# Two standalone norm stages dissolved: statistics in the routing and attention stages, the norm itself inside the zone stages

## The reference, cut to what matters

```python
def _layernorm(x):                       # over the 128 features, no gain, no bias
    return (x - mean(x)) / sqrt(var(x) + 1e-5)

def _L0_ffn_ref(x, W1, b1, W2, b2, Wa, Wb):
    pooled = x.mean(axis=1)              # over the 256 tokens of a sample
    h = tanh(pooled @ W1 + b1)
    probs = softmax(h @ W2 + b2)
    top_p, top_i = top_k(probs, 3)       # 3 of 8 zones for each sample, weights w
    for e in range(8):
        zone_outputs += (gelu(x @ Wa[e]) @ Wb[e]) * w[:, e]
    return x + zone_outputs

x = L0_attn_x                            # 32 samples x 256 tokens x 128 features
x = x + 0.5 * _L0_ffn_ref(_layernorm(x), ...)    # norm_a, route_a, zones_a
x = x + _L0_attn_ref(_layernorm(x), ...)         # splat
x = x + 0.5 * _L0_ffn_ref(_layernorm(x), ...)    # norm_b, route_b, zones_b
x = x + 0.5 * _L1_ffn_ref(_layernorm(x), ...)    # spline_a
x = x + _L1_attn_ref(_layernorm(x), ...)         # causal
x = x + 0.5 * _L1_ffn_ref(_layernorm(x), ...)    # spline_b
```

## Time and profile before

| | us |
|---|---|
| median of 3 runs | 1727.47 (1726.98 to 1727.72) |
| the profiled execution | 1725.12 |
| its span, first to last instruction | 1723.1 |
| PE busy | 1448.0 (84%) |
| DVE busy | 1283.4 (74%) |
| ACT busy | 919.7 (53%) |
| POOL busy | 366.5 (21%) |

### The profile page before, as it was taken

How to read it: one execution, slowest core, us unless ns; L and a number is a source line. 1 busy time by engine, 2 the same in 40 slices (tenths; PEclk the granted TensorE clock), 3 DMA queues, 4 the chain that set the end, 5 groups by cost and what they waited for, 6 DMA issues and landing times. The chain is left out here.

```text
span 1723.1 us, 43799 instructions
## 1 busy us (share of the span) xinstructions
PE 1448.0 (84%) x14174; PEld 1033.6 (60%) x14175; DVE 1283.4 (74%) x2859; ACT 919.7 (53%) x1393; POOL 366.5 (21%) x532
## 2 busy tenths in 40 slices
PE   0023999999699999999999994389999979799797
PEld 0011788888456666666666652178888844499543
DVE  0788777877477777777777766967887879588696
ACT  0112444444266666666666663234444449677597
POOL 5033000000121121111211102400000048522386
PEclk9999999999699999999999996589999989899899
DMA  8000000000000000000000000000000000000011
GB/s 205 8 0 0 1 0 0 0 0 0 1 2 2 0 0 0 0 0 0 0 0 0 2 2 1 0 1 0 0 0 0 0 1 0 1 1 0 1 43 55
DMA packets 20569, 14.14 MB, mean 8 GB/s; under 512 B 7296, under 2 KB 16416, under 8 KB 20512
## 3 DMA queue, kind: packets, MB, share of 16 engines
q1 hardware_dynamic: 16008, 13.14, 2.8%
q10 hardware_dynamic: 3192, 0.15, 0.2%
q0 software_dynamic: 1312, 0.09, 0.1%
HBM read 9.18 MB, written 4.19 MB: 8 GB/s over the span
## 5 line engine op out<-in xcount | busy, mean ns | idle before, releaser
L1217 DVE TENSOR_REDUCE neg_max<-splat_fill_ps 128x2 f16<-128x512 f32 x512 | 334.8, 692 | 112.2 <-PE splat_fill_ps L1004 108.1
L1144 ACT ACTIVATE splat_probs<-splat_ring 128x1024 f32<-128x1024 f32 x256 | 248.1, 1021 | 97.8 <-PE splat_ring L1031 97.8
L814 ACT ACTIVATE zones_a_hidden<-zones_a_hidden_ps,gelu_scale 128x1024 f32<-128x1024 f32 x96 | 107.0, 1115 | 130.2 <-PE zones_a_hidden_ps L764 130.2
L814 ACT ACTIVATE zones_b_hidden<-zones_b_hidden_ps,gelu_scale 128x1024 f32<-128x1024 f32 x96 | 107.0, 1115 | 129.8 <-PE zones_b_hidden_ps L764 129.8
L1031 PE MATMUL splat_ring<-splat_queries,splat_keys 32*128 32x256 f32 x2048 | 152.5, 392 | 4.1 <-ACT splat_probs L1144 3.2
L1004 PE MATMUL splat_fill_ps<-splat_keys,splat_queries 32*128 32x256 bf16 x1024 | 146.0, 279 | 6.1 <-DVE neg_max L1217 3.2
L1045 PE MATMUL splat_mixed_ps<-splat_probs,values 128*32 128x256 f32 x2048 | 137.0, 385 | 0.4 <-ACT splat_probs L1144 0.4
L1290 POOL TENSOR_TENSOR splat_square<-splat_linear 128x512 f32<-128x512 f32 x32 | 33.3, 1042 | 449.8 <-ACT splat_linear L1158 449.8
L845 DVE SCALAR_TENSOR_TENSOR zones_b_hid_lo<-zones_b_hidden,unit_scale,zones_b_hid_hi 128x1024 f16<-128x1024 f32 x96 | 123.3, 1284 | 3.4
L845 DVE SCALAR_TENSOR_TENSOR zones_a_hid_lo<-zones_a_hidden,unit_scale,zones_a_hid_hi 128x1024 f16<-128x1024 f32 x96 | 123.3, 1284 | 3.4
L762 PE MATMUL zones_a_hidden_ps<-norm_hi,wa_hi 128*128 (+1 forms) x384 | 105.8, 276 | 3.3 <-issue 3.2
(11 more groups left out here) (341 smaller groups left out, 3385.3 us busy)
## 6 DMA issues: line engine op xcount, KB each, us to landing
out<-x_res SPq DMA_DIRECT2D x16, 256.0 KB, 2.3
stage_a<-L_ffn_Wa SPq DMA_DIRECT2D x1, 2048.0 KB
qkv_rows<-L_attn_qkv_w SPq DMA_DIRECT2D x1, 192.0 KB
attn_w<-L_attn_W SPq DMA_DIRECT2D x1, 192.0 KB
deltas<-L_attn_splat_deltas ACTq DMA_DIRECT2D x6, 0.5 KB
log_scales<-L_attn_splat_log_scales POOLq DMA_DIRECT2D x6, 0.5 KB, 6.3
centers<-L_attn_splat_centers SPq DMA_DIRECT2D x6, 0.5 KB
log_amps<-ttn_splat_log_amplitudes SPq DMA_DIRECT2D x6, 0.5 KB
```

The lines of the kernel that those rows point to most:

```text
L814: nc.scalar.activation(hidden[k][:, :, :], hidden_ps[k][:, :, :], ACT.Gelu_apprx_tanh, scale=s.gelu_scale[:, :]).then_inc(gelu_done, 1)
L1144: nc.scalar.activation(probs[u % PROB_BUFFERS][:, :, :, :].rearrange("p h k i -> p (h k) i"), ring[u % 2][:, :, :], ACT.Exp).then_inc(exp_ ...
L1217: nc.vector.tensor_reduce(s.neg_max[:, tile, t:t + 2, GROUP * g + SPLATS], fill_ps[f % 2][:, :, :], AX.X, ALU.max, negate=True).then_inc(m ...
```

## The change

- The stages norm_a and norm_b are gone, with `norm_hi`, `norm_lo` and `pooled` for all samples.
- Statistics: in route_a, DVE takes them for all 64 tiles in four parts of 8 samples, and POOL makes mean and 1/std of 16 tiles at a time (`Moments`, `few=8`). For zones_b they are taken in the splat stage: DVE takes those of sample b - 2 in slot b, right behind the statistics of sample b + 4, and POOL makes the power and copies mean and 1/std to `s.mean` and `s.rstd`.
- `route` computes the token sums by PE: for each of the 64 tiles a float32 matmul with the x tile (128x128) as stationary and one column of 1/std as moving operand, and two matmuls with a matrix of ones for the shift. ACT copies the sums from PSUM, and the hidden layer takes two matmuls.
- `zones`: three samples ahead, ACT norms the two tiles of a sample by one Identity activation each (scale 1/std, bias -mean/std, both one value for each partition). POOL takes half of that and adds it to x, in two instructions. PE transposes the normed tiles two samples ahead (`turn`), ACT keeps the high part (`keep_high`), DVE the low part (`keep_low`). DVE's add of the result to x also waits for POOL's add to those rows. The output of first_product has two PSUM buffers instead of three.
- The loop of the splat stage starts at slot 5 instead of 2.

```diff
+def settle(engine, semaphore, value):
+
+    if isinstance(value, int):
+        wait(engine, semaphore, value)
+        return
+    value = engine.to_reg(value)
+    engine.wait_ge(semaphore, 1)
     engine.wait_ge(semaphore, value)
...
-def zone_norm(nc, s, stage):
...
+class Moments:
...
+    def statistics(self, dve, n):
+        rows = self.s.x_res[:, n * self.tiles:(n + 1) * self.tiles, :]
+        for t in range(self.tiles):
+            last = self.nc.vector.bn_stats(self.stats[n % 2][:, t, :], rows[:, t, :])
+        last.then_inc(self.stats_ready, 1)
+        dve.wait_ge(self.stats_ready, n + 1)
+        wait(dve, self.rstd_ready, n - 1)
+        for t in range(self.tiles):
+            last = self.nc.vector.bn_aggr(self.moments[n % 2][:, t, :], self.stats[n % 2][:, t, :])
+        last.then_inc(self.moments_ready, 1)
+
+    def power(self, pool, n):
+        nc, s = self.nc, self.s
+        columns = slice(n * self.tiles, (n + 1) * self.tiles)
+        pool.wait_ge(self.moments_ready, n + 1)
+        wait(pool, self.rstd_ready, n)
+        nc.gpsimd.tensor_copy(s.mean[:, columns], self.moments[n % 2][:, :, 0])
+        nc.gpsimd.tensor_tensor(self.shifted[:, :], self.moments[n % 2][:, :, 1],
+                                s.eps[:, 0:1].to_broadcast([P, self.tiles]), ALU.add).then_inc(self.shifted_ready, 1)
+        pool.wait_ge(self.shifted_ready, n + 1)
+        nc.gpsimd.tensor_tensor(s.rstd[:, columns], self.shifted[:, :],
+                                s.minus_half[:, 0:1].to_broadcast([P, self.tiles]),
+                                ALU.pow).then_inc(self.rstd_ready, 1)
+
+
+def route(nc, s, stage, few=0):
...
+        moments = Moments(nc, s, ctx, stage, few) if few else None
+        parts = SAMPLES // few if few else 1
...
+            @block.gpsimd
+            def _(pool):
+                for n in range(parts if few else 0):
+                    moments.power(pool, n)
+
             @block.tensor
             def _(pe):
-                nc.tensor.matmul(hidden_ps[:, :], s.router_w1[:, :], s.pooled[:, :],
-                                 start=True, stop=True).then_inc(hidden_in, 1)
+
+                for n in range(parts):
+                    if few:
+                        pe.wait_ge(moments.rstd_ready, n + 1)
+                    for b in range(n * SAMPLES // parts, (n + 1) * SAMPLES // parts):
+                        for t in range(TILES):
+                            row = TILES * b + t
+                            nc.tensor.matmul(pooled_ps[:, 0, b:b + 1], s.x_res[:, row, :], s.rstd[:, row:row + 1],
+                                             start=(t == 0), stop=(t == TILES - 1))
+                pe.wait_ge(products_ready, 1)
+                for t in range(TILES):
+                    last = nc.tensor.matmul(pooled_ps[:, 1, :], s.all_ones[:, :],
+                                            s.shift[:, :].rearrange("p (b t) -> p t b", t=TILES)[:, t, :],
+                                            start=(t == 0), stop=(t == TILES - 1))
+                last.then_inc(pooled_in, 1)
+                pe.wait_ge(pooled_ready, 1)
+                for n in range(2):
+                    last = nc.tensor.matmul(hidden_ps[:, :], s.router_w1[:, :], pooled[:, n, :],
+                                            start=(n == 0), stop=(n == 1))
+                last.then_inc(hidden_in, 1)
...
+                act.wait_ge(pooled_in, 1)
+                nc.scalar.activation(pooled[:, :, :], pooled_ps[:, :, :], ACT.Copy).then_inc(pooled_ready, 1)
...
+                for n in range(parts if few else 0):
+                    moments.statistics(dve, n)
+                if few:
+                    dve.wait_ge(moments.rstd_ready, parts)
+                nc.vector.scalar_tensor_tensor(s.shift[:, :], s.mean[:, :], -1.0, s.rstd[:, :],
+                                               ALU.mult, ALU.mult).then_inc(products_ready, 1)
...
-        hidden_ps = [ps(f"{stage}_hidden_ps{i}", [P, CHUNKS, TOKENS]) for i in range(TOP_K)]
+        turned = [ps(f"{stage}_turned{i}", [P, TOKENS]) for i in range(2)]
+        hidden_ps = [ps(f"{stage}_hidden_ps{i}", [P, CHUNKS, TOKENS]) for i in range(2)]
...
+                def take_half(b, parity):
+                    rows = tile_of(s.x_res, b)
+                    pool.wait_ge(norm_ready, b + 1)
+                    wait(pool, x_ready, b)
+                    nc.gpsimd.tensor_tensor(half[:, :, :], normed[parity][:, :, :],
+                                            s.half[:, 0:1].unsqueeze(2).to_broadcast([P, TILES, P]),
+                                            ALU.mult).then_inc(half_ready, 1)
+                    settle(pool, half_ready, b + 1)
+                    nc.gpsimd.tensor_tensor(rows, rows, half[:, :, :], ALU.add).then_inc(x_ready, 1)
+
+                take_half(0, 0)
+                take_half(1, 1)
+                with pairs(pool, 2, SAMPLES) as i:
+                    for parity in range(2):
+                        take_half(i + parity, parity)
...
+                def turn(b, parity):
+                    pe.wait_ge(norm_ready, b + 1)
+
+                    wait(pe, norm_parts, b - 1)
+                    for t in range(TILES):
+                        last = nc.tensor.transpose(turned[parity][:, t * P:(t + 1) * P], normed[parity][:, t, :],
+                                                   s.ident32[:, :])
+                    last.then_inc(norm_turned, 1)
+
+                def first_product(u, b, zone, k, of, to):
+
+                    wait(pe, gelu_done, u - 1)
+                    if k == 0:
+                        pe.wait_ge(norm_parts, b + 1)
+                    x_hi, x_lo = norm_hi[of][:, :], norm_lo[of][:, :]
...
+                            first_product(u + 2, b if k == 0 else b + 1, chosen[k + 2], (k + 2) % TOP_K,
+                                          parity if k == 0 else 1 - parity, (parity + k) % 2)
                         second_product(u, b, k, parity, chosen[k])
+                        if k == 0 and turns:
+                            turn(b + 2, parity)
                         if k == 1 and not is_first:
                             turn_back(b - 1, 1 - parity)
...
+                def norm(b, parity):
+                    settle(act, norm_turned, b - 1)
+                    settle(act, half_ready, b - 1)
+                    for t in range(TILES):
+                        column = bass.ds(b * TILES + t, 1)
+                        last = nc.scalar.activation(normed[parity][:, t, :], tile_of(s.x_res, b, t), ACT.Identity,
+                                                    bias=s.shift[:, column], scale=s.rstd[:, column])
+                    last.then_inc(norm_ready, 1)
+
+                def keep_high(b, parity):
+                    act.wait_ge(norm_turned, b + 1)
+                    nc.scalar.activation(norm_hi[parity][:, :], turned[parity][:, :], ACT.Copy).then_inc(norm_high, 1)
+
+                def gelu(u, k, of):
                     act.wait_ge(first, u + 1)
                     wait(act, split, u - TOP_K + 1)
-                    nc.scalar.activation(hidden[k][:, :, :], hidden_ps[k][:, :, :], ACT.Gelu_apprx_tanh,
+                    nc.scalar.activation(hidden[k][:, :, :], hidden_ps[of][:, :, :], ACT.Gelu_apprx_tanh,
...
+                    if turns:
+                        keep_high(b + 2, parity)
+                    if norms:
+                        norm(b + 3, 1 - parity)
+
+                norm(0, 0)
+                norm(1, 1)
+                keep_high(0, 0)
+                keep_high(1, 1)
+                norm(2, 0)
...
+                def keep_low(b, parity):
+                    dve.wait_ge(norm_high, b + 1)
+                    nc.vector.tensor_tensor(norm_lo[parity][:, :], turned[parity][:, :], norm_hi[parity][:, :],
+                                            ALU.subtract).then_inc(norm_parts, 1)
...
+                    dve.wait_ge(x_ready, b + 1)
...
                         split_unit(TOP_K * b + k, b, k)
-                        if k == 2 and not is_first:
-                            add(b - 1, 1 - parity)
-
+                    if turns:
+                        keep_low(b + 2, parity)
+                    if not is_first:
+                        add(b - 1, 1 - parity)
...
+        ended = RowNorm(nc, s, ctx, stage + "_ended", 0, DEEP)
...
-            for b in range(FIRST, LAST):
+            for b in range(FIRST, LOOP):
                 slot(b, b % DEEP)
-            with engine.Fori(LAST, SAMPLES - 6 - (DEEP - 1), DEEP) as i:
+            with engine.Fori(LOOP, SAMPLES - 6 - (DEEP - 1), DEEP) as i:
                 for n in range(DEEP):
-                    slot(i + n, (LAST + n) % DEEP)
+                    slot(i + n, (LOOP + n) % DEEP)
             for b in range(SAMPLES - 6, SAMPLES + LAST):
...
                         statistics(b + 4, after)
+                    if there(b, -2):
+
+                        settle(dve, added, b - 1)
```

(14 more changed lines are left out.)

136 lines of the change are left out of this document (56 added, 80 removed).

## The result

| us | before | after |
|---|---|---|
| median | 1727.52 (1726.98 to 1727.72) | 1666.67 (1665.73 to 1668.71) |
| the profiled execution | 1725.12 | 1665.73 |
| its span | 1723.1 | 1663.9 |

What follows compares the result with a forecast made beforehand. DVE alone bounds the norm stages, PE the zone stages and splat. Gains 29.7 + 36.8 - 16.0 = 50.5 us; 1725.1 - 50.5 = 1674.6, median 2.4 above: 1677.0, range 1650 to 1712.

Steps and rivals of the forecast that it cites:

- Part 1: norm_a and route_a: the router's Tanh starts at 136.9 instead of after the table load's end at 166.6, gaining 29.7 us.
- the mis-sized term: Token sums on PE: each instruction costs 0.23 us, set by the weight load, so 128 take 29.4 us.
- The four loads in 0.93: Four weight loads at the kernel's start took 0.93 us, read as 0.23 us for each token-sum instruction.
- part 2: splat and route_b: statistics move into splat, Tanh of route_b at 1084.3 against 1121.05, gaining 36.8 us.
- The rival (0.13 at full clock): Token sums get the full clock, 0.13 us an instruction: gains 74.5 in all, 1653; chance 0.26 for full or partly full clock.
- Part 2, splat: Splat slots: the added statistics, 1.1 us of DVE work a slot, make nothing late, cost 0.
- 1.5 us of cover: Splat slot: DVE's maxima end at 709.67, PE refills their buffers only at 711.2, leaving 1.5 us for added work.
- the rival of 33 us without cover: Splat slots: if the maxima come later than 711.2, 33 us come back, giving 1710; chance 0.07.
- Part 3: Both zone stages: PE's added transposes cost 6.4 us a stage and the start 1.6, together 8.0 each, 16.0 for both.
- POOL at nothing: Zone stages: POOL's two added operations hold up DVE at a cost of 0, bounds 0 and 0.6 us a sample.
- Slower than before: Token sums: load and matmul run one behind the other at 0.70 us an instruction, 120 us back, 1797; chance 0.04.

Runs made afterwards that it cites:

- the last run: Changed kernel with token sums turned round (x tile moves, 32 columns loaded), route_a in eight parts, early table load and filler matmuls: 1644.8 us, ratio to before 0.9529.

## Why the prediction was right, and where it was off

*What bounds the kernel.* Held: both norm stages came off the path, the zone stages grew by what PE was given, splat didn't change.

*Part 1.* 32.8 instead of 29.7, with Tanh 37.8 us behind the first statistics instead of 40.9. First product after 7.9 us, not 8.7. The 128 instructions took 27.3, not 29.4; that is the mis-sized term. The four loads in 0.93 are a busy time that includes the last load's end; from start to start it is 0.21. The same term is 2.1 of the 2.5 us of part 2 (39.3 instead of 36.8); the 2.7 us forecast from the end of the add (1050.0) to the start of route_b (1052.7) were 2.6.

*The clock.* The value was chosen as that of a half clock, with the earlier trace rows as the reason, and the runs bear that out: the sums don't raise the clock, and it falls when it was up. But the earlier trace rows also has norm_a at 1.00, and the prediction passed over it. It is the same blank as in route_a after, and the two rows say so by themselves: 64 instructions of the same kind took 21.95 us at the 1.00 and 21.94 at the 0.50. The rival (0.13 at full clock) had its price too high for the same reason as the forecast: 0.112. Its condition was not given in the kernel after; in the last run it was, though with the product turned round, and gave 12.7 us in route_b, near the 13.2 of that rival. (Its Tanh at 126.1 is 0.4 less than its terms add up to.)

*Part 2, splat.* Nothing was late: 609.38 against 609.58. Right in the sum, wrong in the reason: 1.5 us of cover was far too narrow a reading, and the rival of 33 us without cover had no ground.

*Part 3.* 7.7 and 8.1 instead of 8.0 each. Between `zone_code` and the first product it is 3.2 us instead of 1.6, as forecast; the other 6.1 us of zones_a are the 60 transposes of the samples behind the first two, 0.109 each or 6.5, less what the clock gives back by rising 3.6 us into the products instead of 4.9. POOL at nothing: shown by taking its work away.

*What was not in the sum.* The kernel before, once more:

> The kernel before once more, for the spread of its stretches. In the trace of before the first statistics start at 96.0 us, in five traces of the changed kernel and its variants at 93.4 to 94.2. If the change shortens the preparation, the start is again near 96.0; if it is the spread of the loads, it can fall anywhere from 93 to 97. The stretches behind it should repeat: norm_a and route_a 78.0, zones 263.2 and 262.7, splat 609.6, norm_b and route_b 78.9.

Its stretches repeat: 78.05 us to `zone_code` of route_a, zone stages 263.3 and 263.1, norm_b and route_b 78.9, and splat 610.5. Its first statistics are at 95.8. So 2.65 us of the difference lie ahead of all that was changed: DVE's first reading of the loaded zone weights starts at 49.0 instead of 51.6. Before, two traces have 51.3 and 51.6, the kernel after and ten of its variants 48.9 to 49.9, and the last version, which holds another 128x2080 tile, 51.3. What differs is how fast the same loads come in. The stretch from 10 to 20 us, before and after, with GB/s as the last number:

```profile
10.00:20.00 10.00, 0.00 (x0) 0.00 (x0) 0.00 (x0) 0.00 (x0) 10.00 (x20) 1.00 1.15 224
```

```profile
10.00:20.00 10.00, 0.00 (x0) 0.00 (x0) 0.00 (x0) 0.00 (x0) 10.00 (x20) 1.00 1.11 285
```

It is 224 in both traces of before, 229 in the last version, and 264 to 285 in the eleven others. So in these traces it goes with the kernel. Where the tiles lie in SBUF is one candidate; it was not tried.

*Slower than before* (serial products at 0.70) fell with the first row: a load of 0.33 us starts every 0.214.

So of the 8.6 us by which the spans differ more than forecast, 4.2 are the 0.23 that was 0.2135, 2.65 the loads, 1.4 shorter steps around the sums, and 0.4 the rest. Of the 10.3 between the forecast and the median, 1.5 more are that the profiled execution lies 0.9 below its median, where the forecast had taken 2.4.

## What to carry to other kernels

Price an instruction by the distance from start to start in a run of them, and note beside it which clock it was taken at. In these traces the column of the clock says nothing ahead of its first entry: compare the duration of a known matmul there with one at a recorded clock. The room for added work on an engine is the sum of its idle time ahead of the operation that would be late, over the loop, and a run that adds twice the work shows it at once. And where a product has a wide and a narrow operand, try both ways round: loading 128 float32 columns to move one cost 0.2135 us at the clock that these sums got, loading 32 and moving 128 cost 0.109 at the clock that those got.

## What was unexpected in the hardware

- Float32 weight loads set the pace in long runs of small matmuls: 128 columns 0.2135 us an instruction at half clock and 0.112 at full, whether 1 or 32 columns moved; 32 columns with one moving 0.053 at half clock; 128 columns of float16 0.025 at full clock. The Trainium skill (TensorE: Matmul & The Clock Gate, section "LDWEIGHTS (loading the stationary operand)") has the load grow with the columns, and its formula makes 107 ns for 128, an estimate; the float32 rows agree on the growth (a quarter of the price for 32 columns) and are near it at full clock (0.112), but at half clock it is twice that.
- PE was recorded busy for 19 us on end at a granted clock of 0.50 in the sums with one moving column, also after 8.7 us of other work ahead of them; with x as the moving operand, and 32 columns loaded, the record stayed at 1.00 to the end of the sums.
- Two engines that wait for each other's instructions can stretch each other by 16 to 93% (DVE's two by 32 and 16, POOL's product by 93) with hardly a trace in the total, as long as neither is the bound.
